# Seven block products in place of eight for q, k and v, all attention as one stage, and its output through DRAM

## The chip, the cores and the metric

The kernel runs on one core of one Trainium2 chip. The metric is device time in microseconds (us) of one execution. A core has five instruction streams: PE (TensorE, matrix products), DVE (VectorE), ACT (ScalarE), POOL (GpSimd) and SP (SyncE, which here only issues DMAs). Each works its own list in order and waits on semaphores for the others.

## The reference, cut to what matters

32 sequences of 64 tokens, 1024 features, everything in fp32. `_L0_cond_ref` is a 1024x1024 linear layer plus a LoRA adapter by sequence; its result is c below.

```python
# c = x @ W.T + b + adapter                       (2048 tokens x 1024)
q = _rope((c @ wq).reshape(B, S, 32, 128), pos)   # 32 query heads
k = _rope((c @ wk).reshape(B, S, 8, 128), pos)    # 8 key heads
v = (c @ wv).reshape(B, S, 8, 128)
scores = einsum('bqhgd,bshd->bhgqs', q grouped by 4, k) * 128 ** -0.5
attn = softmax(where(causal, scores, lowest))
out = einsum('bhgqs,bshd->bqhgd', attn, v).reshape(B, S, 4096)
x = x + out @ wo
# then, on x: a second conditioned layer, and an FFN with routed adapters
x = x + _L0_ffn_ref(_L0_cond2_ref(x, ...), ...)
```

## The kernel before, in words

**Precision.** PE takes fp32r operands of reduced precision. Each fp32 factor is therefore split in two: a high part (a copy into fp32r) and a low part (the factor minus the high part). Every product is three matmuls into one PSUM bank, W_hi X_hi + W_hi X_lo + W_lo X_hi, in `three` (lines 542 to 544). Activations lie with features on partitions, so one "product" of a weight block is 128 output features by 512 tokens.

**Stages.** After a short stage that folds weights, a loop over two halves of 1024 tokens runs four stages:

1. turn x and split it; at the same time POOL puts the residual into the tile `x1` (line 1196);
2. W1: 8 blocks of 128 features make c. ACT writes c_hi from PSUM (L1016), DVE writes c_lo from PSUM (L1349);
3. a loop over 8 groups (one key head, one value head, four query heads each). Per group PE forms 12 products of 8 x 3 matmuls (2 for k, 2 for v, 8 for q) and then 32 products of 2 x 3 matmuls for the output projection of this group, which DVE adds to `x1` (L1457);
4. the second conditioned layer and the FFN.

**A group.** The weights come through two tiles `raw`: SP loads 512 KB, ACT copies the high part (L999), POOL subtracts for the low part (L1205), ten times a group. DVE turns k and q (`rotate`: L1381 times cosine, L1384 times sine in two half-partition pieces, both read PSUM; L1388 adds the two SBUF tiles). The attention of a group has four units (two pairs of heads by two halves of the tokens). A unit is: scores on PE (L719), mask, row maximum and subtraction on DVE (L1394 to L1399), exponent on ACT, sum, reciprocal and multiplication on DVE (L1406 to L1410), a transpose on PE (L729), a copy on ACT, P times V on PE (L741), and the split of the result into `o_hi` (ACT) and `o_lo` (DVE). The units are placed between products by hand (`SCORE_AT`, `TURN_AT`, `PV_AT`), some of them in the output projection. The order of every engine is thus written out in the code; semaphores only delay it.

Of the kernel before, what the change touches and what calls it, by code (L numbers as in the profile page):

```python
# [42 lines left out]
P = 128  # L43
# [49 lines left out]
PER_G = 10  # L93
# [16 lines left out]
Q_H, Q_C = 0, TT  # L110
Q_G = Q_C + TT * KC
Q_PER_G = 12 + 32
# [12 lines left out]
H_G = H_C + 3 * KC - 1  # L125
H_X1 = H_G + 8 * NKV
# [6 lines left out]
def raw_count(r):  # L133

    return 16 * (r // 2 + 1)


SCORE_AT = {7: 0, 8: 1, 11: 2, 12: 3}
TURN_AT = {8: 0, 9: 1, 12: 2, 13: 3}
PV_AT = {9: 0, 10: 1, 13: 2, 14: 3}  # L140
# [5 lines left out]
def build(nc, x, ids1, ids2, W1, b1, A1, B1, wq, wk, wv, wo, W2, Wr2, A2, B2, Wf, bf, Af, Bf, Rf, consts,  # L146
          gates_d, m_d, c2_d, t_d, out):
    assert D == TOK and KC == TB
    with ExitStack() as ctx:
# [14 lines left out]
        CL = sb("c_lo", [P, KC * TOK], F32R)  # L164
        XR = sb("x_raw", [P, TB * D], offset=0)
# [8 lines left out]
        OH = sb("o_hi", [P, GQ * TOK], F32R, offset=64 * KB)  # L174
        OL = sb("o_lo", [P, GQ * TOK], F32R, offset=80 * KB)
        K = sb("k_rot", [P, TOK], offset=96 * KB)
        V = sb("v_tok", [P, TB * HD], offset=100 * KB)
        VT = sb("v_feat", [P, NT], offset=104 * KB)
        Q = sb("q_rot", [P, 4 * NT], offset=106 * KB)
        SM = sb("probs", [P, 2 * NT], offset=114 * KB)  # L180
        PT = sb("probs_t", [P, NT], offset=118 * KB)
        RC = sb("rope_cos", [P, 2 * NT], offset=120 * KB)
        RS = sb("rope_sin", [P, 2 * NT], offset=124 * KB)
# [4 lines left out]
        X1 = sb("x1", [P, KC * TOK])  # L188
        TW_IN, TW_OUT = ([X1[:, (h + r) * D:(h + r + 1) * D] for r in range(4)] for h in (0, 4))

        RAW = [sb(f"raw{i}", [P, D]) for i in range(2)]
        WH = [sb(f"w_hi{i}", [P, D], F32R) for i in range(2)]
        WL = [sb(f"w_lo{i}", [P, D], F32R) for i in range(2)]
# [10 lines left out]
        OS = [sb(f"out_s{t}", [P, NT], offset=buf + (4 + 2 * t) * KB) for t in range(TT)]  # L204
        BC = [sb(f"lora_b{i}", [P, TT * P]) for i in range(2)]
        CT = sb("consts_sb", [P, C_COLS])
# [8 lines left out]
        LG = sb("logits", [P, TB * EF])  # L215
        PR = sb("route_p", [P, TB * EF])
        GA = sb("gate_a", [P, TB * EF])
        M8 = sb("top8", [P, TB * 8])
        I8 = sb("top8_i", [P, TB * 8], U32)
# [4 lines left out]
        RCP = sb("row_rcp", [P, 2 * SPT])  # L224
        assert BASE + at[0] <= nc.SBUF_PARTITION_SIZE_BYTES, at[0]
# [48 lines left out]
        x_res = sem("x_res")  # L274
        qk_in = sem("qk_in")
# [11 lines left out]
        o_split = sem("o_split")  # L287
# [27 lines left out]
        def o_view(o, w, par):  # L315

            pair = o[:, (w // 2) * 2 * TOK:(w // 2 + 1) * 2 * TOK]
            return pair.rearrange("p (h t b s q) -> p t s b h q", h=2, t=TT, b=BPT, s=2)[:, w % TT, par]
# [20 lines left out]
        def _(sp):  # L339
# [63 lines left out]
            with sp.Fori(0, HALVES) as hf:  # L403
# [21 lines left out]
                def load_w1_first():  # L425
# [6 lines left out]
                    for j in range(2):  # L432
                        load(j, t_d[TW_W + j])
# [14 lines left out]
                for n in range(TT * SPT):  # L448
                    t, n8 = n // SPT, n % SPT
                    m = adapter(n)  # L450
                    sp.dma_start(B1S[n8 * RANK1:(n8 + 1) * RANK1, t * D:(t + 1) * D],
                                 B1[bass.ds(m * RANK1, RANK1), :]).then_inc(b1_in, 16)
                with sp.Fori(1, KC // 2) as i:
                    for s in range(2):

                        sp.wait_ge(split_w, w_base + i * 2 + (S_W + s - 2 + 1 + 2))
                        load(s, t_block(i * 2 + (TW_W + s)))
# [3 lines left out]
                with sp.Fori(0, NKV) as g:  # L461
                    dg = sp.snap(d_base + g * PER_G)

                    def col(w, c):
                        return w.rearrange("(k p) n -> p k n", p=P)[:, :, bass.ds(c, P)]

                    srcs = [col(wk, g * P), col(wv, g * P)]
# [1249 lines left out]
```

## Time and profile before

| | |
|---|---|
| median of 3 runs | 2875.87 us (2873.94 to 2877.47) |
| the profiled execution | 2878.1 us, of it 2876.3 us span |
| PE busy | 2827.7 us, 98%, 13944 matmuls |
| DVE busy | 1482.6 us, 52% |
| ACT busy | 498.2 us, 17% |
| POOL busy | 485.2 us, 17% |
| granted PE clock, mean | 0.996 |

Busy time is the time in which an engine worked; the span is the time from the first to the last instruction. Idle time of an engine costs something only if another one waits for it. "x1024" is a count, "128x512" is partitions by elements.

### The profile page before, as it was taken

What the parts mean: (1) busy time and instruction counts of PE and PEld (TensorE: products, weight loads), DVE (VectorE), ACT (ScalarE), POOL (GpSimd) and SP (SyncE); (2) the same over time, 40 slices, a digit from 0 to 9 for tenths busy, and PEclk for the clock granted to TensorE, in tenths of its full rate; (3) what the DMA queues carried; (4) which work ended last, traced back from release to release, by engine and by line L of the source; (5) the groups of instructions that cost most, each with busy time, mean ns of one, the idle gap of its engine ahead of it and who ended that gap; (6) DMA issues with size and microseconds to landing.
All of it is one profiled execution on the core that took longest, in us unless ns stands there. A gap on an engine that the chain in (4) does not pass through costs nothing.

```text
span 2876.3 us, 37235 instructions
## 1 busy us (share of the span) xinstructions
PE 2827.7 (98%) x13944; PEld 2321.0 (81%) x13944; DVE 1482.6 (52%) x2187; ACT 498.2 (17%) x657; POOL 485.2 (17%) x198
## 2 busy tenths in 40 slices
PE   8989999999999999999998999999999999999999
PEld 7867888888888888878877788888888888887887
DVE  2131556465655646565523255646556564656452
ACT  2122112111111211131202211112111111212110
POOL 0020212112111211210303021111112111221030
PEclk9999999999999999999999999999999999999999
DMA  6841111111111111101442111111111111110232
GB/s 209 234 137 37 45 44 36 44 43 43 37 44 44 41 46 36 44 29 60 109 136 73 44 44 37 44 44 36 44 44 44 40 40 44 37 43 29 80 94 69
DMA packets 230717, 174.57 MB, mean 61 GB/s; under 512 B 65146, under 2 KB 198394, under 8 KB 230658
## 3 DMA queue, kind: packets, MB, share of 16 engines
q1 hardware_dynamic: 202850, 151.77, 18.1%
q10 hardware_dynamic: 27808, 22.02, 2.4%
q8 instruction: 36, 0.59, 0.1%
q14 instruction: 23, 0.19, 0.0%
HBM read 151.55 MB, written 22.22 MB: 60 GB/s over the span
## 4 chain that ended last, share of the span: by engine, by line
PE 89%; DVE 7%; issue 3%; ACT 1%; DMA 0%; SPq 0%; DVEq 0%; ACTq 0%
PE prod L542 27%; PE prod L544 26%; PE prod L543 26%; PE turned L741 2%; DVE x L1457 2%; PE turned L719 2%; PE turned L536 1%; PE prod L638 1%; PE prod L904 1%; PE turned L729 1%; DVE row_max L1397 1%; DVE rope_sin L1384 1%; DVE row_sum L1406 1%; DVE probs L1394 1%; PE turned L709 0%
## 5 line engine op out<-in xcount | busy, mean ns | idle before, releaser
L542 PE MATMUL prod<-c_hi,w_hi 128*128 128x512 f32 (+1 forms) x1856 | 735.0, 396 | 3.2 <-DVE c_lo L1468 3.2
L544 PE MATMUL prod<-c_hi,w_lo 128*128 128x512 f32 (+1 forms) x1856 | 723.7, 390 | 0.0
L543 PE MATMUL prod<-c_lo,w_hi 128*128 128x512 f32 (+1 forms) x1856 | 722.7, 389 | 0.0
L1205 POOL TENSOR_TENSOR w_lo<-raw,w_hi 128x1024 fp32r<-128x1024 f32 x160 | 389.0, 2431 | 1785.5 <-ACT w_hi L999 1785.5
L1457 DVE TENSOR_TENSOR x<-prod,x 128x512 f32<-128x512 f32 x512 | 345.9, 689 | 268.9 <-PE prod L544 268.9
L542 PEld LDWEIGHTS prod<-c_hi,w_hi 128*128 128x128 f32 (+1 forms) x1856 | 347.4, 187 | 79.2 <-DVE c_lo L1468 4.0
L544 PEld LDWEIGHTS prod<-c_hi,w_lo 128*128 128x128 f32 (+1 forms) x1856 | 347.3, 187 | 75.6
L542 PE MATMUL prod<-o_hi,w_hi 128*128 128x512 f32 x1024 | 405.7, 396 | 0.0
L543 PEld LDWEIGHTS prod<-c_lo,w_hi 128*128 128x128 f32 (+1 forms) x1856 | 347.7, 187 | 71.4 <-issue 1.0
L544 PE MATMUL prod<-o_hi,w_lo 128*128 128x512 f32 x1024 | 399.1, 390 | 0.0
L543 PE MATMUL prod<-o_lo,w_hi 128*128 128x512 f32 x1024 | 398.8, 389 | 0.0
L1381 DVE TENSOR_TENSOR rope_cos<-prod,consts_sb 128x512 f32<-128x512 f32 x160 | 110.7, 692 | 407.7 <-PE prod L544 405.8
L542 PE MATMUL prod<-x_hi,w_hi 128*128 128x512 f32 x656 | 283.7, 432 | 4.4 <-DVE x_lo L1236 1.7
L999 ACT CAST w_hi<-raw 128x1024 fp32r<-128x1024 f32 x160 | 168.4, 1052 | 677.3 <-PE prod L544 677.3
L544 PE MATMUL prod<-x_hi,w_lo 128*128 128x512 f32 x656 | 257.6, 393 | 0.0
L543 PE MATMUL prod<-x_lo,w_hi 128*128 128x512 f32 x656 | 257.0, 392 | 0.0
L542 PEld LDWEIGHTS prod<-o_hi,w_hi 128*128 128x128 f32 x1024 | 192.2, 188 | 42.7
L544 PEld LDWEIGHTS prod<-o_hi,w_lo 128*128 128x128 f32 x1024 | 192.2, 188 | 41.1
L543 PEld LDWEIGHTS prod<-o_lo,w_hi 128*128 128x128 f32 x1024 | 192.3, 188 | 38.1
L1384 DVE TENSOR_TENSOR rope_sin<-prod,consts_sb 64x512 f32<-64x512 f32 x320 | 220.3, 689 | 4.2
L542 PEld LDWEIGHTS prod<-x_hi,w_hi 128*128 128x128 f32 x656 | 123.8, 189 | 42.7 <-issue 17.6
L543 PEld LDWEIGHTS prod<-x_lo,w_hi 128*128 128x128 f32 x656 | 123.8, 189 | 37.2 <-issue 13.9
(123 smaller groups left out, 2209.9 us busy)
## 6 DMA issues: line engine op xcount, KB each, us to landing
raw<-in_wq SPq DMA_DIRECT2D x64, 512.0 KB, 4.0
raw<-in_wo SPq DMA_DIRECT2D x64, 512.0 KB, 3.7
raw<-t_scratch SPq DMA_DIRECT2D x34, 512.0 KB, 3.5
t_scratch<-x ACTq DMA_DIRECT2D x17, 512.0 KB, 4.9
x_raw<-in_x SPq DMA_DIRECT2D x16, 512.0 KB, 8.2
raw<-in_wk SPq DMA_DIRECT2D x16, 512.0 KB, 3.5
raw<-in_wv SPq DMA_DIRECT2D x16, 512.0 KB, 3.6
raw<-m_scratch SPq DMA_DIRECT2D x16, 512.0 KB, 3.5
```

Source lines behind the costliest of these rows:

```text
L536: mm = pe.transpose(TP[par][:, c * P:c * P + rows], raw[0:rows, c * P:(c + 1) * P], ident[0:rows, 0:rows])
L542: pe.matmul(dst, wh, xh, start=start, stop=False)
L543: pe.matmul(dst, wh, xl, start=False, stop=False)
L544: return pe.matmul(dst, wl, xh, start=False, stop=stop)
L638: pe.matmul(PJ[(first + t) % 4][:], BC[s][:, t * P:(t + 1) * P], HM[:, t * NT:(t + 1) * NT], start=False, stop=True).then_inc(prod, 1)
L719: mm = pe.matmul(SCB[:, b * SEQ:(b + 1) * SEQ], Q[:, t * 2 * NT + b * P:t * 2 * NT + (b + 1) * P], K[:, t * NT + b * SEQ:t * NT + (b + 1) ...
L741: mm = pe.matmul(OB[par][:, b * P:(b + 1) * P], V[rows, (t * BPT + b) * HD:(t * BPT + b + 1) * HD], PT[rows, b * P:(b + 1) * P], start=Tru ...
L999: act.copy(WH[j % 2][:], RAW[j % 2][:]).then_inc(wd_hi, 1)
L1205: pool.tensor_tensor(WL[j % 2][:], RAW[j % 2][:], WH[j % 2][:].bitcast(F32), ALU.subtract).then_inc(split_d, 1)
L1381: dve.tensor_tensor(view(RC[:, rs], SPT), src, cos, ALU.mult)
L1384: ins = dve.tensor_tensor(view(RS[a:a + hd2, rs], SPT), src[b:b + hd2], sin, ALU.mult)
L1457: dve.tensor_tensor(X1[:, xs], PJ[q % 4][:], X1[:, xs], ALU.add).then_inc(taken, 1)
```

## The change

**The identity.** The weights are taken in pairs of 128-column blocks: (k, v), (q0, q1), (q2, q3), so 3 pairs a group and 24 a half. For a pair the 256 x 1024 weight is a 2 x 2 grid of blocks (input features in two halves, two heads), and c is a 2 x 2 grid (input features in two halves, tokens in two halves). Eight block products would give the four outputs; seven give them too if sums and differences of blocks are multiplied (P1 to P7), and their results are combined by additions (U2, C11, U3, C22, C21, C12). A block product has 4 x 3 matmuls, so a pair has 84 in place of 96.

**Sums of c**, once a half: T1, T2 (in the memory of `x1`) and T4, made by DVE and split by ACT and DVE. W1 now writes c as fp32 (ACT, L1278), ACT copies the high part from it (L1285) and DVE subtracts from SBUF. W1's blocks run in the order 0, 4, 1, 5, 2, 6, 3, 7. The residual is stored to DRAM first (8 DMAs) and loaded again after the last pair.

**Sums of weights**, each pair, on POOL: five additions or subtractions and seven low parts, all 128x512. ACT copies seven high parts. Each of the seven products has its own slot (hi and lo), refilled for the next pair once its product is done.

**Combining**, on DVE: five additions a pair. P2 accumulates on P1's bank, P7 on P6's, P3 on P5's; ACT copies P1 out first, into `p_sum`. The rotation (`turn`) reads PSUM for the first output and SBUF for the others, 64x1024 at a time for C22 and C21 together.

**Attention** runs one pair behind, with units placed at fixed products. Its output goes to DRAM by a DMA that ACT issues (`o_store`). **The output projection** of all 8 groups comes behind, with that output loaded again; the last two or three units stand between its first products (`TAIL`).

The diff, cut to its core:

```diff
-PER_G = 10
+PER_G = 4
+BANK = {P1: 2, P6: 3, P2: 2, P5: 1, P7: 3, P4: 0, P3: 1}
+OPENS = (P1, P6, P5, P4)
@@ SP
+                for b in range(TB):
+                    sp.wait_ge(x_res, hf * TB + (b + 1))
...
+                    sp.dma_start(view(x1_d, KC)[:, :, b * P:(b + 1) * P], view(X1[:], KC)[:, :, b * P:(b + 1) * P]
+                                 ).then_inc(x1_out, 16)
                 with sp.Fori(1, KC // 2) as i:
...
@@ PE
-                    for j in range(12):
-                        bank_free(Q_G + j, qg)
-                        main(Q_G + j, (j // TT) % 2, j % TT, CH, CL).then_inc(prod, 1)
-                        if j in (3, 4):
-                            turn_v(j - 3)
-                        attention(j)
+                def attention(B, lp, n):
+                    if lp % 3 != Q01 and lp >= 2:
+                        e = 4 * ((lp - 1) // 3) + 2 * (lp % 3 == KV)
+                        if n == 1:
+                            score(B, e)
+                        if n == 3:
+                            score(B, e + 1)
+                        if n == 5:
+                            turn_p(B, e)
+                        if n == 6:
+                            pv(B, e)
+                    if lp % 3 != Q23 and lp >= 3:
+                        e = 4 * ((lp - 2) // 3) + 2 * (lp % 3 == Q01)
+                        if n == 0:
+                            turn_p(B, e + 1)
+                        if n == 1:
+                            pv(B, e + 1)
+                    if lp % 3 == Q01 and n in (2, 3):
+                        turn_v(B, lp // 3, n - 2)
+                def pair(B, lp):
+                    for n in range(NP):
+                        attention(B, lp, n)
...
+                        pe.wait_ge(s_lo, B["s_lo"] + (NP * lp + n + 1 + 14))
+                        if n == P2:
+                            pe.wait_ge(p1_in, B["p1s"] + (lp + 1))
+                        else:
+                            last = {P1: C11 - NC, P6: U3 - NC, P5: C12 - NC, P4: C21 - NC, P7: U2, P3: C22}[n]
+                            pe.wait_ge(comb, B["comb"] + (NC * lp + last + 6))
+                        for k in range(4):
+                            xh, xl = operand(n, k)
...
+                            mm = three(PJ[BANK[n]][:], slot_hi(n)[:, ks], slot_lo(n)[:, ks], xh, xl,
+                                       n in OPENS and k == 0, k == 3, skip=True)
@@ ACT
+                for n in (P2, P5, P7, P4):
+                    weight_hi(B0, 0, n)
+                act.wait_ge(t4_step, hf * 4 + 3)
+                act.copy(T4H[:], T4LF[:]).then_inc(t4_hi, 1)
+                weight_hi(B0, 0, P3)
+                def p1_copy(B, lp):
+                    act.wait_ge(a_prod, B["a_prod"] + (NP * lp + P1 + 1))
+                    act.wait_ge(comb, B["comb"] + (NC * (lp - 1) + U3 + 6))
+                    act.copy(P1S[:], PJ[BANK[P1]][:]).then_inc(p1_in, 1)
@@ POOL
+                    add(S2F[:], a21, a11, ALU.subtract)
+                    add(S2F[:], S2F[:], a22, ALU.add)
+                    lo(P1, a11)
+                    lo(P6, S2F[:])
+                    lo(P2, a12)
+                    add(SLF[P5][:, NT:2 * NT], a21, a22, ALU.add, P5)
+                    lo(P5, SLF[P5][:, NT:2 * NT])
+                    add(SLF[P7][:, NT:2 * NT], a11, a21, ALU.subtract, P7)
+                    lo(P7, SLF[P7][:, NT:2 * NT])
+                    lo(P4, a22)
+                    add(SLF[P3][:, NT:2 * NT], a12, S2F[:], ALU.subtract, P3)
+                    lo(P3, SLF[P3][:, NT:2 * NT])
@@ DVE
+                    def turn(n, out, x, segs, c, signal, value):
...
+                        for a, b in ((0, hd2), (hd2, 0)):
...
+                            dve.tensor_tensor(view(rs[a:a + hd2, :], segs), x[b:b + hd2], sin, ALU.mult)
+                        dve.tensor_tensor(out, x, cos, ALU.mult).then_inc(signal, 1)
+                        dve.wait_ge(signal, value)
+                        dve.tensor_tensor(out, out, view(rs, segs), ALU.add).then_inc(qk_in, 1)
...
+                    formed(P4)
+                    combined(C22)
+                    dve.tensor_tensor(b0, b0, bank[P4], ALU.subtract).then_inc(comb, 1)
+                    if kind != KV:
+                        combined(C21)
...
+                        turn(1, both, view(CB[:, 2 * NT:4 * NT], TT * SPT), TT * SPT, 0, roped, r_of(B, lp, 1))
+                    formed(P3)
+                    dve.tensor_tensor(a1, a1, bank[P3], ALU.add).then_inc(comb, 1)
+                    combined(C12)
+                    turn(1 if kind == KV else 2, dst[1], view(a1, SPT), SPT, 0, roped,
+                         r_of(B, lp, 1 if kind == KV else 2))
```

**Where instructions move.** First DVE, at a query head. Before, one head's rotation for 512 tokens and then the mask; `prod` is a PSUM bank, the other names are in SBUF.

```order
L1381 TENSOR_TENSOR rope_cos<-prod,consts_sb 128x512
L1384 TENSOR_TENSOR rope_sin<-prod,consts_sb 64x512 x2
L1387 REGISTER_ALU
L1388 TENSOR_TENSOR q_rot<-rope_cos,rope_sin 128x8x64
L1394 TENSOR_TENSOR probs<-turned,consts_sb 128x512
```

Now, on DVE at the end of a pair of query heads, from the combination C21 on; `combined` is in SBUF.

```order
L1942 TENSOR_TENSOR combined<-combined,prod 128x512
L1903 TENSOR_TENSOR rope_sin<-combined,consts_sb 64x1024 x2
L1905 TENSOR_TENSOR q_rot<-combined,consts_sb 128x16x64
L1907 TENSOR_TENSOR q_rot<-q_rot,rope_sin 128x16x64
L1948 TENSOR_TENSOR combined<-combined,prod 128x512
L1903 TENSOR_TENSOR rope_sin<-combined,consts_sb 64x512 x2
L1905 TENSOR_TENSOR q_rot<-combined,consts_sb 128x8x64
L1907 TENSOR_TENSOR q_rot<-q_rot,rope_sin 128x8x64
L1858 TENSOR_TENSOR probs<-turned,consts_sb 128x512
```

Eight rotation instructions for the last three outputs of the pair now stand behind one another, all but the two combinations with both inputs in SBUF, and the mask of the next unit stands behind them. Second POOL, in a group; before, ten rows like these two:

```order
L1205 TENSOR_TENSOR w_lo_76<-raw_72,w_hi_74 128x1024
L1205 TENSOR_TENSOR w_lo_77<-raw_73,w_hi_75 128x1024
```

Now, on POOL for one pair (three of these in a group; slots 94 to 100 are P1, P6, P2, P5, P7, P4, P3):

```order
L1590 TENSOR_TENSOR s_f_141<-raw_89,raw_88 128x512
L1590 TENSOR_TENSOR s_f_141<-s_f_141,raw_89 128x512
L1595 TENSOR_TENSOR slot_94<-raw_88,slot_94 128x512
L1595 TENSOR_TENSOR slot_95<-s_f_141,slot_95 128x512
L1595 TENSOR_TENSOR slot_96<-raw_88,slot_96 128x512
L1590 TENSOR_TENSOR slot_f_104<-raw_89 128x512
L1595 TENSOR_TENSOR slot_97<-slot_f_104,slot_97 128x512
L1590 TENSOR_TENSOR slot_f_105<-raw_88,raw_89 128x512
L1595 TENSOR_TENSOR slot_98<-slot_f_105,slot_98 128x512
L1595 TENSOR_TENSOR slot_99<-raw_89,slot_99 128x512
L1590 TENSOR_TENSOR slot_f_107<-raw_88,s_f_141 128x512
L1595 TENSOR_TENSOR slot_100<-slot_f_107,slot_100 128x512
```

POOL's share of a group went from 6 instructions of 1024 elements for q, k, v to 36 of 512. Third ACT, where W1 ends. Before, ACT goes from c_hi of the last block straight to the group's weights; now, from the last c on:

```order
L1278 ACTIVATE c_lo_f<-prod,bias_128 128x512
L1285 CAST c_hi<-c_lo_f 128x512
L1261 CAST slot_96<-raw_88 128x512
L1261 CAST slot_97<-slot_f_104 128x512
L1261 CAST slot_98<-slot_f_105 128x512
L1261 CAST slot_99<-raw_89 128x512
L1332 CAST t_hi<-t_lo_f 128x2048
L1261 CAST slot_100<-slot_f_107 128x512
L1340 COPY p_sum<-prod 128x512
```

The copy of P1, for which PE's third product P2 waits, stands behind all high parts of the first pair and behind T4.

## Rows read from the trace of the kernel before


**Rows 1.** Page: span, engines, moved GB/s in 40 slices
```profile
span 2876.3 us, 37235 instructions
...
PE 2827.7 (98%) x13944; PEld 2321.0 (81%) x13944; DVE 1482.6 (52%) x2187; ACT 498.2 (17%) x657; POOL 485.2 (17%) x198
...
GB/s 209 234 137 37 45 44 36 44 43 43 37 44 44 41 46 36 44 29 60 109 136 73 44 44 37 44 44 36 44 44 44 40 40 44 37 43 29 80 94 69
```

**Rows 2.** Chain of waits, the same place one group apart: start us, us, what
```profile
987.88 1.91 issue
1113.13 1.91 issue
```

**Rows 3.** Timeline of PE, two matmuls with two between them: start us, us
```profile
1022.40 0.39 PE L542 MATMUL prod<-o_hi,w_hi 128*128 128x512 f32 x1
1023.09 0.39 PE L542 MATMUL prod<-o_hi,w_hi 128*128 128x512 f32 x1
```

**Rows 4.** Chain of waits inside one group: start us, us, what
```profile
1059.29 0.44 PE turned L709 x4
1082.01 1.73 PE turned L719 x16
1091.01 0.45 PE turned L729 x4
1097.39 1.09 PE turned L741 x16
1098.48 0.43 PE prod L542
```

**Rows 5.** Groups by line and shape: count, busy us, mean ns, idle before
```profile
L1205 POOL TENSOR_TENSOR w_lo<-raw,w_hi 128x1024 fp32r<-128x1024 f32 x160 | 389.0, 2431 | 1785.5 <-ACT w_hi L999 1785.5
L1384 DVE TENSOR_TENSOR rope_sin<-prod,consts_sb 64x512 f32<-64x512 f32 x320 | 220.3, 689 | 4.2
L1399 DVE TENSOR_TENSOR probs<-probs,row_max 128x512 f32<-128x512 f32 x64 | 44.3, 692 | 2.2
L1108 ACT CAST c_hi<-x 128x512 fp32r<-128x512 f32 x32 | 17.7, 617 | 5.4 <-DVE x L1457 5.4
L1408 DVE RECIPROCAL row_rcp<-row_sum 128x8 f32<-128x8 f32 x64 | 13.0, 203 | 2.2
L1210 POOL TENSOR_TENSOR w_lo<-small_folded,w_hi 128x704 fp32r<-128x704 f32 x2 | 3.4, 1720 | 16.4 <-ACT w_hi L1102 16.4
```

**Rows 6.** Timeline of DVE around one POOL instruction: start us, us
```profile
1050.58 2.05 DVE L1388 TENSOR_TENSOR k_rot<-rope_cos,rope_sin 128x512 f32<-128x512 f32 x1
1067.36 0.69 DVE L1388 TENSOR_TENSOR q_rot<-rope_cos,rope_sin 128x512 f32<-128x512 f32 x1
```

**Rows 7.** Timeline of POOL, same stretch
```profile
1049.68 2.40 POOL L1205 TENSOR_TENSOR w_lo<-raw,w_hi 128x1024 fp32r<-128x1024 f32 x1 [8.49 <-ACT w_hi L999]
```

**Rows 8.** Line 1388: ns min/median/max of its instructions
```profile
L1388 DVE TENSOR_TENSOR q_rot<-rope_cos,rope_sin x128: 691/693/2051, 315.7 to 2598.1; 128x512 f32<-128x512 f32 x128
```

**Rows 9.** Timeline of POOL, gates multiplied: eight together
```profile
1370.36 24.79 POOL L1221 TENSOR_TENSOR g_f<-g_f,h_twice 128x1024 f32<-128x1024 f32 x8 [90.45 <-DMA g_f<-gates_scratch]
```

**Rows 10.** Timeline of DVE in the same stretch
```profile
1373.87 6.64 DVE L1488 TENSOR_TENSOR x_lo<-g_f,x_hi 128x1024 fp32r<-128x1024 f32 x2
1380.43 0.74 DVE L1482 SCALAR_TENSOR_TENSOR x<-prod,biasf,x 128x512 f32<-128x512 f32 x1
1381.10 2.76 DVE L1488 TENSOR_TENSOR x_lo<-g_f,x_hi 128x1024 fp32r<-128x1024 f32 x1
```

**Rows 11.** Timeline of SP at the start of W1
```profile
188.92 24.10 SPq L412 DMA_DIRECT2D raw<-t_scratch  x4
```

**Rows 12.** Timeline of DVE at the start of W1: 1024 elements, two SBUF inputs
```profile
198.61 1.23 DVE L1308 TENSOR_TENSOR w_lo<-raw,w_hi 128x1024 fp32r<-128x1024 f32 x1 [0.19 <-ACT w_hi L977]
```

**Rows 13.** Timeline of ACT: c of block 1, its end
```profile
209.62 0.69 ACT L1016 ACTIVATE c_hi<-prod,bias 128x512 fp32r<-128x512 f32 x1 [5.66 <-PE prod L638]
```

**Rows 14.** Busy time by stretch: PE, PEld, DVE, ACT, POOL, PEclk, DMA, GB/s
```profile
155.00:180.00 25.00, 17.03 (x86) 14.03 (x85) 13.74 (x10) 10.17 (x10) 18.92 (x8) 0.86 0.58 125
180.00:268.00 88.00, 87.13 (x360) 67.07 (x359) 19.42 (x22) 18.05 (x28) 2.14 (x1) 1.00 0.17 53
1512.00:1540.00 28.00, 21.74 (x104) 18.30 (x105) 15.80 (x13) 10.86 (x10) 18.83 (x8) 0.76 0.43 81
```

## What the change is expected to do

> **What bounds the kernel now.** I read the page first: PE is busy 98% of the span with 13944 matmuls, so fewer matmuls should mean less time, as long as PE stays fed [rows 1]. Then the chain of waits, for the period of a group: 1113.13 - 987.88 = 125.25 us [rows 2]. Then the timeline of PE: three 128x512 matmuls take 0.68 us, so one costs 0.227 us [rows 3]. A group has 12 x 24 + 32 x 6 = 480 of them, 108.8 us. The rest is the attention's own work on PE: 4 scores of 1.73, 4 transposes of 0.45, 4 P times V of 1.09 with a matmul behind them that takes 0.43 in place of 0.23, and 2 transposes of v of 0.44, together 14.8 us [rows 4]. That leaves 1.6 us of waiting. Last I read the rows by shape, for the unit costs of DVE, ACT and POOL [rows 5], and the timelines of DVE and POOL side by side [rows 6, 7, 9, 10]. POOL works 17% of the span [rows 1], so a meeting of the two is rare now.
>
> **What is removed.** Per pair 96 - 84 = 12 matmuls, per half 24 x 12 = 288, in both halves 576; at 0.227 us that is 131 us. This is all that the change can give on PE: attention and output projection keep their matmuls. PE's work in the stage, per half: pairs 24 x 84 x 0.2267 = 457.0; projection 8 x 192 x 0.2267 = 348.2; attention 8 x 14.8 = 118.4; together 923.6, against 8 x 125.25 = 1002.0 before.
>
> **The unit costs of what is added.** DVE: 0.69 us for 512 elements a partition, also on 64 partitions [rows 5], and 1.23 for 1024 [rows 12]; a reciprocal 0.20 [rows 5]. ACT: 0.62 for a 512-wide copy to fp32r [rows 5]. POOL has no 512-wide row. 1024 elements take 2.40 when undisturbed [rows 7], 704 take 1.72 [rows 5]. The straight line through both gives 1.32 for 512, strict proportion 1.20; a fixed cost could make it 1.40. I take 1.32, since both rows are the same kind of instruction. POOL then has 36 x 1.32 = 47.5 us a group.
>
> **DVE and POOL don't run side by side here.** L1388 adds two SBUF tiles in 0.69 us when POOL is idle. Started at 1050.58 while POOL's subtraction ran until 1052.08, it took 2.05 us: it ended 0.55 us after POOL did [rows 6, 7]. The line's instructions are 0.691 or up to 2.051 us [rows 8]. Where both have much to do, they alternate: eight POOL multiplications take 24.79 us in place of 8 x 2.40 = 19.2, and two DVE subtractions of two SBUF tiles take 6.64 us in place of 2.4 [rows 9, 10]. L1482 right between, with one input in PSUM, takes 0.74 [rows 10], and L1384 keeps its 0.689 on average of 320 [rows 5]: those are not held. (The Trainium skill, "SBUF — State Buffer", section "Who interferes with whom", says the same: a VectorE instruction with two SBUF inputs and a GpSimd instruction that reads SBUF exclude each other for the whole instruction. By its rule the sum below stands; without it the time would be that of the first rival.)
>
> The change makes this meeting permanent. In a group DVE has, with both inputs in SBUF: 3 + 12 rotation instructions of 512, 8 of 1024, and 8 subtractions and multiplications of the softmax, 23 x 0.69 + 8 x 1.23 = 25.7 us. With POOL's 47.5 that is 73.2 us which can't overlap, against 57.1 + 14.8 = 71.9 us of PE. Both are near a tie, and the order of the code adds waits:
>
> - *Score of the first unit.* It needs the double rotation of the pair before. From the end of P4: C21 0.69 + 4 x 1.23 = 5.6 us; PE has P3 and the next P1, 5.44. Undisturbed, PE hardly waits. But POOL always has an instruction ready, so each of the four is held by one, 4 x 1.32 = 5.3: PE waits 5.4 us.
> - *Score of the third unit.* The same, with a transpose more on PE and about three POOL instructions in between: 5.6 + 4.0 - 5.9 = 3.7; taken as 3.5.
> - *Transpose of the first unit's probabilities.* When the score starts, DVE still has C12 0.7 and the last rotation (2.8, with 3.3 of POOL), then mask to subtraction 2.1, U2 0.6, the rotation from PSUM 2.8, the second unit's mask to subtraction 2.1 (+1.2 of POOL) and the normalisation 1.6: 17.2 us. PE has 2 scores and 4 products, 14.4, and 0.4 of this is hidden. PE waits 2.4.
> - *The third unit's transpose:* one P times V more on PE, 2.4 - 1.3 = 1.1.
>
> Together 12.4 us a group, so a group costs 57.1 + 14.8 + 12.4 = 84.3 in the first part and 43.5 in the projection, 127.8 against 125.25. In a half: 8 x 5.4 + 7 x 7.0 = 92, and 2.5 for the last units in the projection: 94.7.
>
> **The first pairs of a half.** Once W1 ends, DVE makes T4 with three 2048-wide subtractions and additions of SBUF tiles (2.3 each, double a 1024-wide one), alternating with POOL's sums; ACT's high part of P5 waits for a POOL sum, that of P7 too, then it copies T4 (1.9), P3's part, and only then P1, which P2 needs. Counting on: T4's first step starts at 3.4 us, its third ends at 12.9, P7's sum at 14.2, T4's copy at 17.3, P3's part at 19.8, P1's copy at 20.3. PE is done with P1 and P6 at 5.4: it waits 15 us. P4 then waits 1.1 for T4's low part, and the second pair 2.9 and 2.3 for the same queue. 21.4 us a half.
>
> **The rest.** The projection alone: 1.36 us of PE for each 0.69 on DVE, with bank and weights ahead; POOL's meeting with DVE's `o_lo` is within three banks of slack. Nothing is charged, and 0 to 0.5 us a group are open. Residual to DRAM: SP comes to the 8 stores at 188.92 [rows 11]; 4.2 MB at the highest rate that the page shows, 234 GB/s [rows 1], take 18 us, until some 209. The first T1 waits for them, behind it the low part of block 2's weights (1.23), and the load of these weights comes through the same queue. PE is done with block 1 at 209.6 [rows 13]. That is 4 us late in the first half (0 to 10), nothing in the second, where SP is early enough. Clock: around a wait of PE at the start of a half it is granted 0.86 for 25 us and 0.76 for 28 us, and full again afterwards [rows 14]; a wait of 15 us can bring that back. 0.24 x 28 = 6.7 us at most for each; most would fall into waits. 2 each, 4 in all (0 to 13). The loads of weights lie a pair ahead, and o_f32 and the residual arrive before the projection asks: nothing.
>
> **The sum.** A half: 923.6 + 94.7 + 21.4 = 1039.7 against 1002.0, so +37.7; twice +75.4; +4 for the stores, +4 for the clock: +83. The profiled execution took 2878.1 us with 1.8 outside its span: 2961. The median lies 2.2 below it: **2959 us**. With POOL at 1.20 the sum is about 38 lower, at 1.40 about 30 higher.
>
> **Rivals.**
> *1. The two run side by side (the other side).* If the new 512-wide POOL instructions did not hold DVE, the scores would wait 0.2 us, the rest nearly nothing: 0.4 us a group, and some 14 us in the first pairs. A half is 923.6 + 3.3 + 14 = 941, 61 less than before; 2878 - 122 + 8 - 2 = 2762. For it: PE is 98% busy and the seven products are real. Against it: rows 6 to 10. It decides from the group's waits: below 6.6 us of waiting a group the change is faster.
> *2. Half of the collisions.* If POOL, waiting for ACT's high parts in order, is often idle when DVE rotates, only half of the holds occur: 2.8 + 1.2 + 0 + 0 = 4 us a group and 18 at the start, 28 less a half: about 2830. Anything between this and my sum is possible; the tie lies at 6.6 us.
> *3. It is worse.* POOL (47.5 + 25.7 held) becomes what sets each pair, with 1.40 us or more an instruction and its semaphores on top, or the clock falls with the waits: 3000 to 3050.
> *4. A part of it:* the late residual or the DRAM way of the attention's output stalls W1 or the projection by 10 us and more. It would show by place.
>
> **How the numbers follow.** My case 0.58 (2900 to 3010), rival 3 0.09, rival 2 with all between 0.20 (0.06 slower, 0.03 equal, 0.11 faster), rival 1 0.13. Within 0.2%, 5.8 us, is what can't be told from no change. So faster 0.24, same 0.03, slower 0.73. The range leaves out rival 1 and the far ends: 2820 to 3015; my own case alone is 2900 to 3010.
>
> **What would show it.** Right: q, k, v and attention take about 84 us a group, PE waits before the scores (5 and 3.5 us) and before transposes of probabilities; rotation instructions with two SBUF inputs at 1024 wide take about 2.5 us on average in place of 1.23, and those from PSUM 0.69; POOL is busy over 60% of that stage; the first P2 of a half waits 15 us for ACT's copy; the projection keeps 43.5 us a group. Wrong: double rotations near 1.23 us, or POOL's 512-wide instructions far from 1.32, or waits on DMAs.

## The result and the profile after

| | before | after |
|---|---|---|
| time, median of 4 runs (us) | 2875.36 | 2946.91 |
| ratio, 95% interval | | 1.025 (1.0233 to 1.0268) |
| span of the profiled execution | 2876.3 | 2946.4 |
| PE busy / idle in it | 2827.7 / 48.6 | 2789.3 / 157.1 |
| mean granted clock | 0.996 | 0.962 |

The change makes the kernel 2.5% slower. The forecast was 2959 us. Its end is near by luck: two of its terms are far off and cancel, as the rows show. Times here and below are medians of the executions that ran at the kernel's usual clock; one execution of e12 (3529.56 us, mean granted clock 0.743) is left out.

The page of after [against rows 1]: engines' busy time, then the chain that ended last, by engine.

```profile
span 2946.4 us, 39418 instructions
...
PE 2789.3 (95%) x13368; PEld 2277.5 (77%) x13368; DVE 1800.9 (61%) x2251; ACT 720.6 (24%) x1059; POOL 1120.4 (38%) x678
...
PE 82%; DVE 9%; issue 4%; SPq 2%; POOL 2%; DMA 1%; ACT 0%; DVEq 0%; POOLq 0%; ACTq 0%
```

PE has 576 matmuls less, yet its busy time fell by 38.4 us only, where 131 were expected. What it waits for, in both halves together (us, times, longest):

```profile
PE turned L898 <- DVE q_rot L1907: 82.0, 30, 3.7
PE prod L714 <- ACT p_sum L1340: 26.4, 2, 13.2
...
PE turned L910 <- DVE probs L1876: 4.3, 4, 1.5
```

Scores (L898) wait for the rotations, transposes of probabilities (L910) nearly never. Of the 30 waits before a score, 16 are of 3.1 to 3.7 us (the first unit's) and 14 of 1.7 to 1.9 us (the third's). The chain of waits shows the same score one group apart, as [rows 2] do for before: 687.30 - 602.32 = 84.98 us.

```profile
602.32 3.67 PE turned L898 x16
...
687.30 2.83 PE turned L898 x13
```

The timeline of PE there tells what the waits table doesn't:

```profile
598.26 0.39 PE L716 MATMUL prod<-c_hi,slot 128*128 128x512 f32 x1
602.32 3.67 PE L898 MATMUL turned<-k_rot,q_rot 128*128 128x64 f32 x16 [3.67 <-DVE q_rot L1907]
...
607.18 0.63 PE L714 MATMUL prod<-t_hi,slot 128*128 128x512 f32 x1
607.61 0.63 PE L715 MATMUL prod<-t_lo,slot 128*128 128x512 f32 x1
...
609.19 0.40 PE L716 MATMUL prod<-t_hi,slot 128*128 128x512 f32 x1
```

After 3.67 us without work the score takes 3.67 us where [rows 4] had 1.73, and the matmuls behind it start 0.43 us apart, not 0.23: the lower of the two clock levels. Full speed is back at 609.2. The clock falls like this behind 27 of the 30 waits; behind three of the short ones it stays up, as around 550.85. The windows give the granted clock as the third figure from the end: the start of the half, a group of this stage, the stretch around 550.85, and the projection.

```profile
302.00:312.00 10.00, 3.05 (x7) 2.47 (x8) 0.89 (x2) 4.56 (x6) 8.47 (x7) 0.50 0.24 70
352.00:437.00 85.00, 79.41 (x404) 65.64 (x404) 63.61 (x72) 24.35 (x42) 54.52 (x37) 0.92 0.21 63
550.00:560.00 10.00, 9.15 (x62) 8.00 (x62) 9.16 (x11) 2.84 (x6) 5.35 (x4) 1.00 0.47 142
...
1000.00:1290.00 290.00, 290.00 (x1280) 239.36 (x1279) 185.52 (x242) 54.07 (x55) 64.07 (x26) 1.00 0.29 96
```

DVE's rotation by shape, the whole span, [against rows 5 and 12]:

```profile
L1903 DVE TENSOR_TENSOR rope_sin<-combined,consts_sb 64x1024 f32<-64x1024 f32 x64 | 111.5, 1742 | 4.4
L1903 DVE TENSOR_TENSOR rope_sin<-combined,consts_sb 64x512 f32<-64x512 f32 x96 | 108.1, 1126 | 6.6
L1905 DVE TENSOR_TENSOR q_rot<-combined,consts_sb 128x1024 f32<-128x1024 f32 x32 | 69.1, 2159 | 0.4
L1907 DVE TENSOR_TENSOR q_rot<-q_rot,rope_sin 128x1024 f32<-128x1024 f32 x32 | 67.8, 2117 | 1.1
L1903 DVE TENSOR_TENSOR rope_sin<-prod,consts_sb 64x512 f32<-64x512 f32 x96 | 66.1, 688 | 102.8 <-PE prod L716 102.2
```

The same instruction takes 0.69 us from PSUM (`prod`) and 1.13 from the SBUF tile (`combined`). The four of a double rotation take 2 x 1.74 + 2.16 + 2.12 = 7.8 us in the mean, 2.8 more than 4 x 1.23. But this mean mixes two kinds of instruction. The last double rotation of each half, with no GpSimd instruction beside it, takes 4.95 us; each of the other 30 takes 7.9 to 8.1. In each of those, three of the four are held by 1.0 to 1.1 us (2.2 to 2.3 in place of 1.22), and one by 0.15 at most. DVE and then POOL ahead of the score shown above:

```profile
597.77 2.22 DVE L1905 TENSOR_TENSOR q_rot<-combined,consts_sb 128x1024 f32<-128x1024 f32 x1
600.02 2.17 DVE L1907 TENSOR_TENSOR q_rot<-q_rot,rope_sin 128x1024 f32<-128x1024 f32 x1
```

```profile
599.63 1.48 POOL L1595 TENSOR_TENSOR slot<-slot_f,slot 128x512 fp32r<-128x512 f32 x1 [0.73 <-ACT slot L1261]
601.07 2.25 POOL L1590 TENSOR_TENSOR s_f<-raw,raw 128x512 f32<-128x512 f32 x1
```

They take turns. POOL's first one ends at 601.11, and DVE's q_rot, begun at 600.02, ends 1.08 us later, nearly the whole length that it has alone (1.22). POOL's next one ends 1.13 us after that. A held instruction has begun while the other still runs, so it loses 1.0 us and not the 1.29 of a whole one. POOL's own by shape, the least and the most held:

```profile
L1595 POOL TENSOR_TENSOR slot<-s_f,slot 128x512 fp32r<-128x512 f32 x48 | 61.8, 1288 | 139.1 <-ACT slot L1261 139.1
L1590 POOL TENSOR_TENSOR s_f<-raw,raw 128x512 f32<-128x512 f32 x24 | 48.0, 1999 | 179.9 <-DMA raw<-in_wv 179.9
```

And the first pair of a half, DVE and then PE:

```profile
292.47 3.20 DVE L1837 TENSOR_TENSOR t_hi_f<-t_hi,c_hi 128x2048 f32<-128x2048 f32 x1
```

```profile
308.95 0.79 PE L714 MATMUL prod<-c_hi,slot 128*128 128x512 f32 x1 [13.21 <-ACT p_sum L1340]
```

### The profile page after: what moved, and what is told of

Read it like the earlier page. It is cut to its first block, busy times and chain, and to the rows that moved or that the text cites. A ratio compares the mean times of both kernels' runs of the same rounds, so it can differ in the third digit from the quotient of the medians.

```text
span 2946.4 us, 39418 instructions
## 1 busy us (share of the span) xinstructions
PE 2789.3 (95%) x13368; PEld 2277.5 (77%) x13368; DVE 1800.9 (61%) x2251; ACT 720.6 (24%) x1059; POOL 1120.4 (38%) x678
## 4 chain that ended last, share of the span: by engine, by line
PE 82%; DVE 9%; issue 4%; SPq 2%; POOL 2%; DMA 1%; ACT 0%; DVEq 0%; POOLq 0%; ACTq 0%
PE prod L714 24%; PE prod L716 23%; PE prod L715 23%; PE turned L898 5%; DVE q_rot L1905 2%; DVE q_rot L1907 2%; DVE rope_sin L1903 2%; PE turned L923 2%; PE prod L1145 1%; PE turned L708 1%; PE turned L910 1%; POOL slot_f L1590 1%; DVE combined L1942 1%; SPq L498 1%; POOL slot L1595 1%
## 5 line engine op out<-in xcount | busy, mean ns | idle before, releaser
L1634 POOL TENSOR_TENSOR w_lo<-raw,w_hi 128x1024 fp32r<-128x1024 f32 x64 | 156.9, 2451 | 579.8 <-ACT w_hi L1417 579.8
L714 PE MATMUL prod<-c_hi,slot 128*128 128x512 f32 x768 | 309.9, 404 | 27.5 <-ACT p_sum L1340 26.4
L714 PE MATMUL prod<-c_hi,w_hi 128*128 128x512 f32 (+1 forms) x832 | 327.4, 394 | 3.4 <-DVE c_lo L2023 3.4
L716 PE MATMUL prod<-c_hi,w_lo 128*128 128x512 f32 (+1 forms) x832 | 324.2, 390 | 0.0
L715 PE MATMUL prod<-c_lo,w_hi 128*128 128x512 f32 (+1 forms) x832 | 323.9, 389 | 0.0
L716 PE MATMUL prod<-c_hi,slot 128*128 128x512 f32 x768 | 301.6, 393 | 0.0
L715 PE MATMUL prod<-c_lo,slot 128*128 128x512 f32 x768 | 300.9, 392 | 0.0
L714 PE MATMUL prod<-t_hi,slot 128*128 128x512 f32 x576 | 256.0, 445 | 1.5 <-DVE t_lo L1846 1.5
L1595 POOL TENSOR_TENSOR slot<-slot_f,slot 128x512 fp32r<-128x512 f32 x144 | 200.5, 1393 | 105.4 <-ACT slot L1261 105.4
L715 PE MATMUL prod<-t_lo,slot 128*128 128x512 f32 x576 | 240.2, 417 | 0.0
L716 PE MATMUL prod<-t_hi,slot 128*128 128x512 f32 x576 | 239.3, 415 | 0.0
L898 PE MATMUL turned<-k_rot,q_rot 128*128 128x64 f32 x1024 | 154.0, 315 | 82.0 <-DVE q_rot L1907 82.0
L1903 DVE TENSOR_TENSOR rope_sin<-combined,consts_sb 64x512 f32<-64x512 f32 (+1 forms) x160 | 219.6, 1372 | 10.9
L898 PEld LDWEIGHTS turned<-k_rot,q_rot 128*128 128x128 f32 x1024 | 150.2, 229 | 97.2 <-issue 94.5
```

The source lines that it names most:

```text
L714: pe.matmul(dst, wh, xh, start=start, stop=False, skip_group_check=skip)
L715: pe.matmul(dst, wh, xl, start=False, stop=False, skip_group_check=skip)
L716: return pe.matmul(dst, wl, xh, start=False, stop=stop, skip_group_check=skip)
L898: mm = pe.matmul(SCB[:, b * SEQ:(b + 1) * SEQ], Q[:, t * 2 * NT + b * P:t * 2 * NT + (b + 1) * P], K[:, t * NT + b * SEQ:t * NT + (b + 1) ...
L1595: pool.tensor_tensor(slot_lo(n), src, slot_hi(n).bitcast(F32), ALU.subtract).then_inc(s_lo, 1)
L1634: pool.tensor_tensor(WL[j % 2][:], RAW[j % 2][:], WH[j % 2][:].bitcast(F32), ALU.subtract).then_inc(split_d, 1)
```

## The experiments

PE's busy and idle time of each profile are the measure: all kernels but e2 have the same 13368 matmuls, so a longer busy time is mostly the slow clock, with a slower start behind each wait. Busy and idle add up to the span of the profiled execution. In e6 that one was the fastest of four and lies 11 us below the median, so differences against e6's profile are smaller than those against its time. The edits are cut to what matters, and what stands behind a # in them is a note.

| run | time (us) | against before | PE busy | PE idle |
|---|---|---|---|---|
| after | 2946.91 | 1.025 | 2789.3 | 157.1 |
| e1 GpSimd narrow | 2786.0 | 0.9685 (0.9669-0.9702) | 2705.2 | 78.4 |
| e2 filler ahead of scores | 2899.26 | 1.0081 (1.0064-1.0097) | 2796.6 | 97.4 |
| e3 first copy of P1 early | 2942.83 | 1.0232 (1.0213-1.0251) | 2790.8 | 151.7 |
| e4 scores later | 2913.75 | 1.0125 (1.0108-1.0142) | 2746.3 | 165.0 |
| e5 rotation split | 2970.07 | 1.0329 (1.0312-1.0346) | 2790.0 | 176.7 |
| e6 split, sums in PSUM | 2910.75 | 1.0125 (1.0108-1.0142) | 2763.5 | 134.3 |
| e7 = e6, scores later | 2862.38 | 0.9952 (0.9935-0.9968) | 2717.7 | 144.4 |
| e8 = e7, all steps read PSUM | 2815.74 | 0.9789 (0.9775-0.9802) | 2710.2 | 103.7 |
| **e9 = e8, scores early** | **2780.33** | **0.9664 (0.9651-0.9677)** | 2703.7 | 74.7 |
| e10 = e8, copy of P1 early | 2814.28 | 0.9787 (0.9773-0.98) | 2713.0 | 98.5 |
| e11 = e9, wait at the score | 2965.29 | 1.0308 (1.0291-1.0326) | 2801.5 | 162.6 |
| e12 = e9, wait at the transpose | 2919.18 | 1.015 (1.013-1.0171) | 2761.4 | 156.0 |

**e1, what GpSimd's width costs.**

```diff
-    pool.tensor_tensor(out, x, y, op)
+    pool.tensor_tensor(out[:, 0:cols], x[:, 0:cols], y[:, 0:cols], op)     # cols = 512 if lp == 0 else 64
-    pool.tensor_tensor(slot_lo(n), src, hi, ALU.subtract)
+    pool.tensor_tensor(slot_lo(n)[:, 0:cols], src[:, 0:cols], hi[:, 0:cols], ALU.subtract)
```

> From the second pair of each half on, GpSimd forms the sums and low parts of the weights only 64 columns wide instead of 512 (the rest of these operands keeps the first pair's values, so this run leaves out that part of the computation); every instruction, wait and order stays, and the sums of the later pairs go through the small tile of the second block sum. Theory A (GpSimd's 1.3 us instructions, 15 a pair, exclude VectorE's rotations and with them make the period): the rotation's steps fall from 1.1 and 1.7 us to about 0.7 and 1.2 us, the score waits (82.0 us in 30) nearly vanish, TensorE keeps its clock, and the time falls by the score waits, the transposes' waits and the slow clock behind them: 150 to 190 us, to 2755 to 2800 us. Theory B (the order of TensorE's products and the place of the scores make the waits, GpSimd hardly counts): score waits of more than 2 us stay, and the time falls by less than 40 us.

161 us less, theory A (the kernel leaves out most of GpSimd's columns, so its output is not that of after). The double rotation's first step, where [rows 12] had 1.23:

```profile
L1912 DVE TENSOR_TENSOR rope_sin<-combined,consts_sb 64x1024 f32<-64x1024 f32 x64 | 78.1, 1220 | 4.4
```

Score waits are 7.4 us in place of 82.0, and PE's busy time is 84.1 us shorter with the same matmuls. GpSimd's work is the cause of both, though PE never waits for it in a group. The order of PE's products is not.

**e2, the clock by itself.**

```diff
     if n == 1:
+        for r in range(8 if kind == KV else 16):
+            pe.matmul(SCB, slot_hi(P6)[:, 0:P], CH[:, 0:NT], start=True, stop=True)
         score(B, e)
```

> Ahead of the first score of each pair TensorE does 16 (pair of the third and fourth query head) or 8 (pair of k and v) matmuls of 128x512 more, into the bank that the score then overwrites: 3.6 and 1.8 us of work at full clock in the place where it waited 3.7 and 1.85 us. Half of the score waits are of other sizes and keep part of their wait. Theory A (the clock: the idle time before a score is what lets the granted clock fall, which costs about 3.2 us for each of 30 scores, 96 us in all, and the loop through TensorE sets the period): the waits shrink, the clock stays near 1.0, and the time falls by 50 to 90 us although work was added. Theory B (VectorE and GpSimd's chain of about 84 us a group sets the period whatever TensorE's clock is): the time stays within 20 us, and what the clock gives back turns up as a wait at a later score or transpose.

368 matmuls more, and 48 us less; no wait at a score is left. At 0.227 us they are 83.5 us of work, but PE is busy only 7.3 us longer than in after: 76 us of slow clock are gone. Theory A, just short of its range. The same window of e2 as shown above of after, clock 1.00 in place of 0.92:

```profile
352.00:437.00 85.00, 83.07 (x450) 68.30 (x449) 69.71 (x75) 23.82 (x42) 56.07 (x38) 1.00 0.21 64
```

It also answers theory B: a half's products take 649.9 us in place of 672.2, a group 81 in place of 84, so DVE and POOL can go faster than in after. The slow matmuls were part of the loop: DVE waits for products that come late. 29.5 us of waits turn up at the transposes.

**e3, the first pair.**

```diff
     for n in (P2, P5, P7, P4):
         weight_hi(B0, 0, n)
+        if n == P2: act.copy(P1S[:], PJ[BANK[P1]][:])
```

> In the first pair of each half ScalarE copies the first product right behind the second product's high part, instead of behind all seven high parts. The prediction charged 15 us a half to this copy, and the trace shows a wait of 13.21 us at the third product. Theory A: that wait goes, 13 us a half, with up to 3 us of slow clock behind each: 26 to 32 us less, 2915 to 2921 us. Theory B (VectorE's three sums of 3.2 us and GpSimd's sums for this pair are as late as the copy): the wait moves to the next products of the same pair, and less than 12 us are gained in all.

4 us less, with intervals that overlap: theory B in time. The first pair's P2 no longer waits, but of the 13.2 us in the first half 11.6 remain in three other waits: two of the same pair for GpSimd (1.76 and 2.27), and, further on than theory B put them, 7.56 at the second pair's P2, for the copy of that pair's P1. PE, then ACT just ahead of this copy:

```profile
298.24 0.49 PE L714 MATMUL prod<-t_hi,slot 128*128 128x512 f32 x1 [1.76 <-POOL slot L1598]
...
328.17 0.79 PE L714 MATMUL prod<-c_hi,slot 128*128 128x512 f32 x1 [7.56 <-ACT p_sum L1343]
```

```profile
327.01 0.62 ACT L1261 CAST slot<-slot_f 128x512 fp32r<-128x512 f32 x1 [3.29 <-POOL slot_f L1593]
327.54 0.58 ACT L1343 COPY p_sum<-prod 128x512 f32<-128x512 f32 x1
```

The second copy stands behind a high part that waits for a GpSimd sum. PE's waits for the copies and for GpSimd in these pairs are 24.0 us in both halves together, where the first copy's were 26.4. e10 repeats it on a faster kernel: 1.5 us, again with intervals that overlap, so neither run shows a gain.

**e4, the place of the scores.**

```diff
-    if n == 1: score(B, e)
-    if n == 3: score(B, e + 1)
+    if n == 2: score(B, e)
+    if n == 4: score(B, e + 1)
```

> The two scores that a pair hosts stand one product later in TensorE's order (before the third and the fifth product of the pair instead of before the second and the fourth); all else stays. Theory A (the loop of VectorE and GpSimd sets the period of 84.9 us a group): the scores wait no more, but the probabilities that follow from them are as much later, the transposes wait in their place, and the time stays within 20 us. Theory B (the place of the scores alone makes the wait): 82 us of waits and the slow clock behind them go, and the time falls by 60 to 180 us.

33 us less: neither. The waits moved, as theory A said (13.7 us are left at the scores, and idle time even rose by 7.9 us):

```profile
PE turned L910 <- DVE probs L1876: 81.0, 34, 3.7
```

But PE's busy time fell by 43.0 us. Idle time seems to cost less clock ahead of a transpose than ahead of a score; but the lengths changed as well, to 14 waits of 3.7 us, behind each of which the clock fell, and others of 1.8 at most, behind which it fell once. e11 and e12 test the place alone.

**e5 to e8, the hold.** The rotation is split, then its inputs go to PSUM one after the other.

```diff
     dve.tensor_tensor(b1_, b0, bank[P5], ALU.add)
+    turn(1, dst2[1], view(b1_, SPT), ...)                    # e5: 512 columns, here
-    dve.tensor_tensor(b0, b0, bank[P4], ALU.subtract)
-    turn(1, both, view(CB[:, 2 * NT:4 * NT], TT * SPT), ...)
+    dve.tensor_tensor(bank[P4], b0, bank[P4], ALU.subtract)  # e6: in its bank (and P3's sum in its own)
+    turn(2, dst2[0], view(bank[P4], SPT), ...)
...
-    dve.tensor_tensor(out, x, cos, ALU.mult)
-    dve.tensor_tensor(out, out, view(rs, segs), ALU.add)
+    dve.tensor_tensor(x, x, cos, ALU.mult)                   # e8: over the bank; P5's sum goes to P7's bank
+    dve.tensor_tensor(out, x, view(rs, segs), ALU.add)
```

> In the pairs of the query heads the double rotation of 1024 columns (four instructions of 1.7 to 2.2 us beside GpSimd) is split into two of 512 columns, and the one of the second half's block stands right behind the sum that forms it, ahead of the fourth product's sum. Theory A (the double rotation behind the last sum but one makes VectorE late at every score): the score waits fall from 82 us to under 40, the slow clock behind them goes with them, and the time falls by 30 to 80 us. Theory B (VectorE and GpSimd together are full, wherever the rotation stands; two of 512 columns cost VectorE 5.5 us where one of 1024 cost 4.9 alone): no gain, within 15 us.

23 us more, against both theories. The longest score wait is 4.33 us, and 31.6 us wait at transposes. That more and shorter instructions from SBUF meet GpSimd more often, with the sums of P4 and P3 behind them, fits this (DVE is busy 1836.8 us, after 1800.9), but no run took it apart.

> As the run with the split rotation, and the sums of the fourth and the third product are left in their PSUM banks, so that six of the rotation's steps a pair read PSUM instead of the SBUF tile. Theory A (an instruction of VectorE that reads two SBUF operands is held by GpSimd's, one that reads PSUM is not: 1.13 us against 0.69 in the profile after): those steps fall to 0.69 us, the waits fall below 20 us, and the time falls by 30 to 60 us more than with the split alone. Theory B (the length of those steps comes from VectorE's own work or from what it writes): they keep 1.1 us, and the time is that of the split alone within 10 us.

59 us less than e5, theory A in time; the waits (35.4 at scores, 31.6 at transposes) are above what it gave.

> As the run with the split rotation and the sums in PSUM, with the two scores one product later. Theory A (what is left of the score waits are small ones that one product, 2.6 us, covers, and the probabilities come early enough now): another 10 to 30 us less, near or under the time of the kernel before. Theory B (the probabilities become late, as when the scores alone were moved: 80.9 us of waits at their transposes): no gain, or up to 20 us lost.

48 us less again (36 between the two profiled executions), more than theory A's 30, and the first complete version under before. Theory A's reason is half right: score waits are gone, but 74.1 us wait at transposes, in pieces of at most 2.06 us, with PE's busy time 45.8 us shorter than in e6. Of e7's rotation, what reads PSUM is free and what adds two SBUF tiles is held:

```profile
L1903 DVE TENSOR_TENSOR rope_sin<-prod,consts_sb 64x512 f32<-64x512 f32 x256 | 176.3, 689 | 63.4 <-PE prod L716 51.3
L1907 DVE TENSOR_TENSOR q_rot<-q_rot,rope_sin 128x512 f32<-128x512 f32 x128 | 159.9, 1249 | 4.4
```

> As the run with sums in PSUM and scores later (2862 us), and the last two-SBUF steps of a rotation go as well: the sum of the fifth product is left in the PSUM bank of the seventh, and the product with the cosine is written over the bank, so that the final addition reads PSUM too. Theory A (what still stretches VectorE beside GpSimd is the final addition, 1.26 us in the mean of 63, and the rotation from the SBUF tile, 0.90 and 1.62 us): all rotation steps take 0.69 us, some 60 us of VectorE's time go in 610, and the time falls to 2810 to 2840 us, with waits at the transposes of the probabilities under 30 us. Theory B (the probabilities' waits come from where the scores stand, with the two normalising steps that have two SBUF operands): VectorE gets shorter, but the waits of 76 us stay and the time is within 10 us of 2862.

47 us less, theory A (34.9 us of waits at transposes, a little over its 30). The final addition, now from PSUM, in e8:

```profile
L1915 DVE TENSOR_TENSOR q_rot<-prod,rope_sin 128x512 f32<-128x512 f32 x128 | 88.5, 691 | 4.4
```

> As the run with every rotation step in PSUM, with the scores where the changed kernel has them (before the second and the fourth product). Theory A (with rotations of 2.8 us the last one is ready a product after the last sum, so the early place gives small score waits of under 1.5 us and the probabilities come 2.6 us earlier): the time is within 10 us of the run with the later scores. Theory B (the last rotation is late at the early place in any case, since it can begin only when the last product of the pair before has ended, and first waits of about 1.5 to 2 us stay for 30 scores): 30 to 60 us more than with the later scores.

35 us less than e8: both theories fall. With rotations that aren't held, the early score doesn't wait at all, and the probabilities are in time too. Of the waits at products, scores and transposes of this stage only those of the first pairs (P1's copy again 26.4 us) and of the last units are left:

```profile
PE turned L911 <- DVE probs L1882: 4.3, 4, 1.5
```

So "scores later" gave 33 and 48 us while rotations were held and took 35 when they weren't.

> As the run with every rotation step in PSUM and the scores later, with the first pair's copy of its first product right behind the second product's high part. In the changed kernel this alone gave 4 us of the 26 that its wait showed. Theory A (the rest of the first pair is late by GpSimd's and VectorE's own chain of sums, which the later scores and rotations don't touch): again 2 to 8 us less. Theory B (the rotations' steps held up the rest): 15 us less or more.

Neither range is met (1.5 us), as said under e3.

**e11 and e12, a wait on purpose.**

```diff
+    act.wait_ge(a_prod, ...)                                 # e11: P1 of the pair; e12: P7
+    for r in range(4): act.copy(CB[:, 0:NT], ...)
-    score(B, e)                                              # e12: turn_p(B, e)
+    pe.wait_ge(late, ...); score(B, e)
```

> The fastest run (every rotation step in PSUM, early scores, 2780 us, no wait at a score), with a wait put in on purpose: for the first score of each of the 30 host pairs ScalarE makes four 512-wide copies (0.6 us each, one after the other) when the product before it has ended, and the score waits for the last. TensorE idles some 2.6 us there, 78 us in all. Theory A (a wait right ahead of a score makes the granted clock fall, and that costs about as much again, as the 60 us at waits of 2.29 us show): 130 to 170 us more, PE busy 50 to 90 us longer for the same matmuls. Theory B (the slow clock of the changed kernel was caused by something else, such as its waits of over 3 us or the two waits close together): 75 to 90 us more, PE busy within 15 us.

> The same four copies and the same wait of some 2.6 us, 30 times, at another place: ahead of the transpose of the first unit's probabilities, behind the fifth product of the pair. Theory A (what follows the wait counts: four transposes and a product of 12 wide matmuls instead of a score of 16 matmuls of 64 columns, so the clock holds, as with the 49 waits of up to 2.06 us at transposes, which cost 14 us): 75 to 95 us more, 2855 to 2875 us. Theory B (only the length of the wait counts): the same time as with the wait at the scores, within 15 us.

e11 costs 185 us: 87.9 of idle time and 97.8 of longer busy time. Theory A, somewhat above its range: the clock takes 3.3 us for each wait of 2.9, and the wait is its cause. e12 costs 139: 81.3 idle and 57.7 busy, 1.9 us a wait. That is between its theories: place counts, 46 us here, of them 40 of busy time, but a transpose is no shelter. PE at a wait of e11, and then of e12:

```profile
383.02 3.38 PE L902 MATMUL turned<-k_rot,q_rot 128*128 128x64 f32 x16 [2.90 <-ACT combined L1358]
386.33 2.08 PE L927 MATMUL turned<-probs_t,v_tok 64*128 64x128 f32 x16
...
390.20 0.39 PE L719 MATMUL prod<-t_lo,slot 128*128 128x512 f32 x1
```

```profile
397.86 0.66 PE L914 MATMUL turned<-consts_sb,probs 128*128 128x128 f32 x4 [2.73 <-ACT combined L1358]
398.28 0.47 PE L718 MATMUL prod<-t_hi,slot 128*128 128x512 f32 x1
...
399.29 0.61 PE L719 MATMUL prod<-t_lo,slot 128*128 128x512 f32 x1
...
402.79 1.16 PE L927 MATMUL turned<-probs_t,v_tok 64*128 64x128 f32 x16
```

In e11 the score (3.38 for 1.73) and what follows are slow at once, until 390.2. In e12 the matmuls start 0.23 us apart at first and are slow from 399.3 to 402.8.

## Why the prediction came out near, and which steps failed

The account in PE's time, of after less before. Predicted idle time is 2 x (94.7 + 21.4) for both halves, 4 for the stores, less the 2 x 8 x 1.6 that before had in its groups. Measured, the busy time of e9 less that of before is the matmuls, and that of after less that of e9 (2789.3 - 2703.7, the same matmuls) the clock. The first is somewhat short of 131, since e9 keeps the slow clock of the first pairs (its mean clock is 0.992, that of before 0.996).

| term | predicted | measured |
|---|---|---|
| 576 matmuls less | -131 | -124.0 |
| slow clock | +4 | +85.6 |
| idle time | +210 | +108.5 |
| sum | +83 | +70.1 |

*The direction and its cause were right.* The hold between DVE and POOL [rows 6 to 10] turned a gain into a loss: without it, in e1 and e9, the same seven products end at 2786 and 2780, where the first rival said 2762. The Trainium skill, "SBUF — State Buffer", section "Who interferes with whom", says that a VectorE instruction with two SBUF inputs contends with a GpSimd one that reads SBUF, and that one with at most one SBUF input (outside its two-port modes) does not. The traces agree with both: 1.13 us against 0.69 in the mean for the same instruction with its input in SBUF or PSUM, and 0.69 for the final addition once it reads PSUM.

*The step that failed is the clock term, +4.* I took the low clock of [rows 14] as something that comes with a wait of 15 us at the start of a half and charged 2 us for each. In fact waits of 1.7 to 3.7 us in front of a score bring it too, behind 27 of 30, at some 3.2 us each (85.6 / 27), and e2 and e11 show that the waits are its cause. Rival 3 named this, the clock that falls with the waits, but with longer times. The profile of before could not show it, since its waits in a group are of 1.0 us at most.

*The waits were too large by 101.* First, the hold: I let each of four instructions be held for a whole one of POOL's, 5.3 us; it was 3.1, three of them held by 1.0. That is nearer to the half hold of rival 2, which has waits of 2.8 and 1.2 us and no term for the clock, and so ends at 2830. The scores then waited 3.67 and 1.85 us in place of 5.4 and 3.5. Second, the transposes' waits (2.4 and 1.1) did not come. The slow matmuls between score and transpose hide them, as e2 bears out: without them waits of about 1 us are there. The period of 84.3 us (85.0 measured) was thus right by two errors. Third, the first pairs: 21.4 us a half predicted, 14.7 and 13.2 measured. P1's copy made PE wait 13.2 (15 predicted), T4's low part 1.5 (1.1), and the second pair didn't wait. e3 adds that this wait was no handle: with the first copy early, PE waits for GpSimd's low parts and for the second pair's copy, which GpSimd's sums hold up, nearly as long. T4's three sums, in turns with POOL's, took 9.7 us, as counted (9.5).

*Small terms.* POOL's 512-wide instruction is 1.29 us (1.32), and POOL is busy 54.5 of 85 us in the group above, 64% (over 60). The double rotations' instructions take 1.94 us on average, where 2.5 was the sign. Three matmuls in [rows 3] are 0.69 us apart, not 0.68; the 0.2267 us that I used is right all the same (290 / 1280). Block 2 of W1 waited 2.84 us for its low part in the first half (4) and not in the second. The projection kept its 43.5 us a group: 290 us for 1280 matmuls, none of it idle. No wait on the attention's way through DRAM shows.

## What to carry to other kernels

Before work is handed to GpSimd, list VectorE's instructions with two SBUF operands in the same stage: moving their inputs to PSUM turned +2.5% into -3.4% here, with no instruction less. Price a short, repeated wait of TensorE at its length and the slow matmuls after it: in these runs 0.2 (e7) to 1.1 (e11) times the wait, more when it is long and when small matmuls follow. Where several places could hold a wait, try the place again after each other change: its sign turned between e7 and e9.

## What the runs showed that was not expected

- Work in an idle gap is free and more: 368 matmuls added took 48 us off (e2).
- The same wait, 2.9 us in the mean, cost 3.3 us of clock ahead of 16 matmuls of 64 columns and 1.9 ahead of 4 transposes and wide ones; 48 waits at transposes, none over 2.06 us, cost 14.0 us in all (e7's busy time against e9's), and the clock fell behind three of them only.
- GpSimd is held as well: its 512-wide instruction takes 1.29 us alone and about 2.25 between two held ones of VectorE.
- The mean of a group hides how a hold works: 1.74 us for a half-partition step is a mix of 1.2 and 2.2. A held instruction of 1024 or of 512 elements loses the same 1.0 us (1.22 to 2.2, 0.69 to 1.7), so one split in two (as in e5) can lose twice as much.
- Open: how the clock's fall depends on the wait. In after it fell behind all 16 waits of 3.1 us and more and behind 11 of the 14 of 1.7 to 1.9, in e7 behind 3 of 48 of up to 2.06 at transposes. No run varied the length alone.
